# Bias of a fill as one wide matmul, fused VectorE operations, a late dense layer and a re-planned order in a four-layer graph kernel

## The reference, cut to what matters

```python
# layer 0: pairwise filters, then two dense layers
y = einsum('bjf,bijf->bif', rf, Wf * A)            # Wf: Gaussians of adj -> dense -> softplus -> dense
y = softplus(y @ Wd1 + bd1) - log 2
x = x + y @ Wd2.T + bd2
# layer 1: hyperbolic graph attention over all pairs i, j of a graph
h    = proj(mobius_add(mobius_matvec(W, h), bias))
xloc = logmap(h_i, h_j)                            # for each pair; needs artanh of a norm
att  = sigmoid(silu([logmap(h_i, h_i), xloc] @ w1.T + b1) @ w2.T)
s    = silu([.., sum_j att * xloc * adj] @ mlp_w1.T + b) @ mlp_w2.T + mlp_b2
x    = x + proj(expmap0(silu(logmap0(proj(expmap(s, h))))))
# layer 2: normalised adjacency times x, dense;  layer 3: message passing, dense
```

## Time and profile before

| | |
|---|---|
| runs | 2771.51, 2779.19, 2786.45 us, median 2779.19 |
| profiled execution | 2783.16 us, of which the span is 2781.3 |
| busy share of the span | PE 89%, DVE 80%, ACT 74%, POOL 64%, PEld 44% |
| mean granted clock of TensorE | 0.935 of full speed |

### The profile page before, as it was taken

One profiled execution on the slowest core, in us unless ns is written; L12 is line 12 of the kernel. 1 busy time (PEld: TensorE's weight loads), 2 busy tenths in 40 slices (PEclk: granted clock), 3 DMA queues, 4 the chain that ended last, 5 costly groups with the idle time before them and its releaser, 6 DMA issues. The chain is left out here.

```text
span 2781.3 us, 63446 instructions
## 1 busy us (share of the span) xinstructions
PE 2473.5 (89%) x25488; PEld 1229.5 (44%) x25488; DVE 2236.3 (80%) x3819; ACT 2066.1 (74%) x1938; POOL 1768.6 (64%) x1149
## 2 busy tenths in 40 slices
PE   4899999999999999999985588899898989898973
PEld 2333333333333333333334355455555555555543
DVE  6699898989989899898986756788888787874546
ACT  5888888888888888888853476767667777776641
POOL 0798898889989898898871344454545453555321
PEclk9999999999999999999995699999999999999976
DMA  8799898998989899999921466565555555576520
GB/s 232 172 200 202 194 198 195 201 201 192 203 194 201 193 202 199 196 197 197 199 68 56 86 122 126 100 125 101 126 101 117 106 108 112 104 115 110 75 53 19
DMA packets 312068, 410.29 MB, mean 148 GB/s; under 512 B 91488, under 2 KB 284640, under 8 KB 286688
## 3 DMA queue, kind: packets, MB, share of 16 engines
q1 hardware_dynamic: 311776, 406.23, 69.8%
HBM read 368.38 MB, written 35.65 MB: 145 GB/s over the span
## 5 line engine op out<-in xcount | busy, mean ns | idle before, releaser
L684 POOL TENSOR_TENSOR f_gate<-rfT,f_sq 128x1024 f32<-128x1024 f32 x512 | 1217.7, 2378 | 227.3 <-DVE f_prod L699 153.1
L617 PE MATMUL PS<-f_h,w_W2T 64*64 64x512 f32 x8192 | 998.9, 591 | 10.0 <-PE PS L617 1.9
L699 DVE SCALAR_TENSOR_TENSOR f_prod<-PS,b2l,f_gate 128x1024 f32<-128x1024 f32 x512 | 657.4, 1284 | 146.7 <-PE PS L617 110.9
L1192 ACT ACTIVATE a_silu<-PS,c_att_b 128x1024 f32<-128x1024 f32 x512 | 544.4, 1110 | 218.0 <-PE PS L1022 215.9
L579 ACT ACTIVATE f_h<-PS,c_b 128x1024 f32<-128x1024 f32 x512 | 556.3, 1113 | 167.3 <-PE PS L599 166.5
L691 DVE TENSOR_REDUCE yT<-f_prod 128x16 f32<-128x1024 f32 x512 | 618.8, 1209 | 0.0
L1334 POOL TENSOR_TENSOR a_outer<-a_by_i,a_by_j 128x256 f32<-128x256 f32 x512 | 355.3, 719 | 413.1 <-PE PS L1022 399.8
L617 PEld LDWEIGHTS PS<-f_h,w_W2T 64*64 64x64 f32 x8192 | 341.1, 133 | 561.4 <-issue 437.7
L599 PE MATMUL PS<-f_gauss,W1two 64*64 64x512 f32 x4096 | 546.1, 595 | 7.1 <-ACT f_gauss L566 4.8
L1022 PE MATMUL PS<-a_outer,a_rows 32*128 32x128 f32 x8192 | 395.0, 299 | 121.1 <-ACT a_silu L1192 82.6
L1022 PEld LDWEIGHTS PS<-a_outer,a_rows 32*128 32x128 f32 x8192 | 319.4, 197 | 339.5 <-issue 147.4
(11 more groups left out here) (244 smaller groups left out, 2288.5 us busy)
## 6 DMA issues: line engine op xcount, KB each, us to landing
f_gauss<-in_adj SPq DMA_DIRECT2D x128, 1024.0 KB, 11.6
f_sq<-adj_sq SPq DMA_DIRECT2D x256, 512.0 KB, 8.6
a_rows<-hw_d SPq DMA_DIRECT2D x1024, 64.0 KB
hw_d<-b_xc SPq DMA_DIRECT2D x16, 512.0 KB, 4.3
hw_d<-b_sq SPq DMA_DIRECT2D x16, 512.0 KB, 6.4
b_x<-in_x SPq DMA_DIRECT2D x8, 512.0 KB, 4.0
x_d<-b_x SPq DMA_DIRECT2D x8, 512.0 KB, 7.3
h_d<-b_h SPq DMA_DIRECT2D x8, 512.0 KB, 6.6
```

The source lines that it names most:

```text
L617: PE.matmul(post("message", c)[rows[b], n, :], W2T[rows[k], rows[fh]], hidden(c, n)[rows[k], b, :], start=not second, stop=bool(second)).t ...
L684: GP.tensor_tensor(by_pair(GATE[c % GATE_BUFS][:]), rf, by_pair(squares), ALU.mult).then_inc(s_gate, 1)
L699: V.scalar_tensor_tensor(PR[c % PR_BUFS][:], post("message", c).rearrange("p b n -> p (b n)"), b2l[:, c % 2:c % 2 + 1], GATE[c % GATE_BUFS ...
L1192: A.activation(SI[p % SI_BUFS][:], PS[:, first:first + 2, :].rearrange("p b n -> p (b n)"), ACT.Silu, bias=cols["att_b1"][:]).then_inc(s_s ...
```

## The change

- The filter stage no longer does the last group's dense layer. `flow_stage` does it: 16 matmuls on PE behind the y fills of lead(1) and two softplus activations on ACT behind the square of lead(1); `Wd1two` stays in memory for it.
- In `per_tile_and_bias` one matmul of 512 columns writes the bias of all 4 tiles, and the 4 tiles' matmuls accumulate on it. Its stationary operand is the first column of the identity, broadcast, so it is 128 partitions deep. `ones` shrinks to one column, broadcast where it is used (L1109).
- `series` loses its last addition of 1, which is folded into the operation that follows; `blend` has three operations and no mask buffer, where it had four; the pair chain loses its addition of 1.
- All ticks are new, and `SHIFT` moves single chains of the first and last groups.

```diff
-    posts.append(("layer", GROUPS - 1))
...
-        layer(GROUPS - 1)
...
 FILLS = {
-    "lead": (("y0", 18.875), ("y1", 21.5625), ("t0", 25.8125), ("t1", 25.8125), ("m0", 34.4375),
-             ("m1", 47.875), ("d", 47.875)),
-    "pair": (("h0", 3.1875), ("h1", 3.1875), ("g", 5.5), ("y", 5.5), ("r0", 8.4375), ("r1", 8.4375),
-             ("r2", 8.4375), ("r3", 12.125)),
+    "lead": (("y0", 19.75), ("y1", 19.75), ("t0", 23.4375), ("t1", 23.4375), ("m0", 33.1875),
+             ("m1", 44.4375), ("d", 44.4375)),
+    "pair": (("h0", 5.25), ("h1", 5.25), ("g", 5.25), ("y", 5.25), ("r0", 9.5), ("r1", 9.5), ("r2", 9.5),
+             ("r3", 11.6875)),
...
+SHIFT = {("lead", 0): -4.25, ("lead", 1): 8.875, ("lead", 2): 4.5, ("pair", 0): -3.1875, ("pair", 1): 4.125, ("mix", 6): -0.0625, ("mix", 7): 1.3125, ("last", 5): -0.1875, ("last", 6): -0.75, ("last", 7): 9.5}
...
         def per_tile_and_bias(n, lhs, rhs, bias, h):
             free(n)
+            PE.matmul(bank(n), ident[:, 0:1].broadcast_to([P, P]), bias[:].unsqueeze(1).broadcast_to([P, HALF_GT, P]),
+                      start=True, stop=True)
             for k in range(HALF_GT):
-                PE.matmul(bank(n)[:, k, :], ones[0:1, :], bias[0:1, :], start=True, stop=False)
-                last = PE.matmul(bank(n)[:, k, :], lhs(h * HALF_GT + k), rhs, start=False, stop=True)
+                last = PE.matmul(bank(n)[:, k, :], lhs(h * HALF_GT + k), rhs, start=False, stop=True,
+                                 skip_group_check=True)
...
+        def late_layer():
+            for fh in range(2):
+                for n in range(2):
+                    first = LATE_GROUP * BANK + n * BANK // 2
+                    for graph in range(2):
+                        for m in range(2):
+                            k_rows, m_rows = slice(graph * NODES, (graph + 1) * NODES), slice(m * NODES, (m + 1) * NODES)
+                            last = PE.matmul(PS[m_rows, 2 * graph + n, 0:BANK // 2], Wd1two[k_rows, fh, m_rows],
+                                             yT[k_rows, fh, first:first + BANK // 2], start=fh == 0, stop=fh == 1,
+                                             skip_group_check=True)
+                            if fh:
+                                last.then_inc(s_hb, 1)
...
+            if g == LATE_GROUP:
+                PE.wait_ge(s_hb, 3 + LAYER_PARTS + 2)
...
+            if g == 1:
+                late_layer()
...
+        def late_layer():
+            A.wait_ge(s_hb, 3 + LAYER_PARTS)
+            for graph in range(2):
+                A.activation(yT[:, :, LATE_GROUP * BANK:(LATE_GROUP + 1) * BANK]
+                             .rearrange("p n (t b i) -> p n t b i", b=2, i=NODES)[:, :, :, graph, :],
+                             PS[:, 2 * graph:2 * graph + 2, 0:BANK // 2].rearrange("p n (t i) -> p n t i", i=NODES),
+                             ACT.Softplus, bias=bd1[:]).then_inc(s_hb, 1)
...
-                ts(o, o, 1.0, ALU.add)
...
-            def blend(o, w, q, msk):
-                tt(w, w, o, ALU.subtract)
-                ts(msk, q, SMALL_SQ, ALU.is_ge)
-                tt(w, w, msk, ALU.mult)
-                tt(o, o, w, ALU.add)
+            def blend(o, w, q):
+                stt(w, w, 1.0, o, ALU.subtract, ALU.subtract)
+                stt(w, q, SMALL_SQ, w, ALU.is_ge, ALU.mult)
+                stt(o, o, 1.0, w, ALU.add, ALU.add)
...
-            tt(e1, e1, e2, MU)
+            stt(e1, e1, 1.0, e2, AD, MU)
...
-            yield 24.5
-            ts(bT[:], bT[:], 1.0, AD)
...
-            yield 33.375
+            yield -112.75
             tt(sF("sn3"), sF("n3"), sF("in3"), MU, gives=(f["clamp"], g))
-            yield 59.5625
+            yield -172.9375
             V.wait_ge(f["tanh3"], g + 1)
```

More of the change, by code:

```diff
@@ L662, in pe_program @@
                     ended += 1
-                    if posts[ended][0] == "layer":
+                    if ended < len(posts) and posts[ended][0] == "layer":
                         first_half(begun)
@@ L761, in run @@
     for slot in range(FIRST_SLOT, GROUPS + 3):
-        live += [Paced(chains[c](slot + ahead), slot * TICKS) for c, ahead in AHEAD.items() if 0 <= slot + ahead < GROUPS]
+        live += [Paced(chains[c](slot + ahead), slot * TICKS + SHIFT.get((c, slot + ahead), 0)) for c, ahead in AHEAD.items() if 0 <= slot + ahead < GROUPS]
         for tick in range(TICKS):
@@ L782, in fill_numbers, with flow_stage @@
     return numbers
-def flow_stage(nc, own, PS, d, W, WrlT, W3, rows, cols, ident, ones, same, by_a, by_m, w2sel, yT, norm, bX, d_x):
+def flow_stage(nc, own, PS, d, W, WrlT, W3, rows, cols, ident, ones, same, by_a, by_m, w2sel, yT, norm, bX, d_x, Wd1two,
+               bd1):
     V, A, PE, GP, SP = nc.vector, nc.scalar, nc.tensor, nc.gpsimd, nc.sync
@@ L1108, in pair @@
                 for r in (slice(0, NODES), slice(NODES, P)):
-                    last = PE.matmul(line(num["y"])[r, k * NODES:(k + 1) * NODES], ones[:, 0:NODES], bMX[:, k, r],
+                    last = PE.matmul(line(num["y"])[r, k * NODES:(k + 1) * NODES], ones[:].broadcast_to([P, NODES]), bMX[:, k, r],
                                      start=True, stop=True)
@@ L1517, in lead @@
             tt(sB("d4"), sB("d4"), sB("rstd"), MU)
-            yield -3.0625
+            yield 13.75
             V.wait_ge(b["ln"], g + 1)
             stt(sB("w"), sB("w"), 0.5, sB("zr"), MU, MU)
-            yield -163.3125
-            blend(sB("o"), sB("w"), sB("q"), sB("msk"))
-            yield -176.1875
+            yield -70.75
+            blend(sB("o"), sB("w"), sB("q"))
+            yield 24.875
             tt(sB("o"), sB("o"), sB("z"), MU)
@@ L1611, in pair @@
             ts(bden[:], bden[:], MIN_NORM, MA)
[L1612 removed]
+            yield 5.875
             recip(bden[:], bden[:], gives=(b["den"], g))
[L1614 removed]
+            yield -25.75
             stt(bq[:], bq[:], 0.0, bden[:], MA, MU, gives=(b["q"], g))
[L1616 removed]
+            yield -62.0625
             ts(bT[:], bq[:], 1.0 / 11, MU)
[L1618 removed]
+            for k, at in ((9, -223), (7, -88.5), (5, -265.875), (3, -77.75)):
                 yield at
                 stt(bT[:], bT[:], 1.0 / k, bq[:], AD, MU)
[L1621 to L1623 removed]
+            yield 21.9375
             V.wait_ge(b["z"], g + 1)
@@ L1631, in pair @@
             tt(by[:], by[:], bz[:], MU)
-            yield -36.4375
-            blend(bT[:], by[:], bq[:], bm[:])
-            yield -214.1875
+            yield -42.8125
+            blend(bT[:], by[:], bq[:])
+            yield -188.25
             tt(bT[:], bT[:], bden[:], MU, gives=(b["T"], g))
             tt(bm[:], bT[:], of_pairs(x2_1), MU, gives=(b["m"], g))
-            yield 26.1875
+            yield 31.3125
             stt(U[g % 3][:], bm[:], -1.0, bn[:], MU, MU, gives=(b["U"], g))
@@ L1735, in mix @@
             recip(sF("zi"), sF("zi"))
-            yield -128.125
+            yield -131.375
             series(sF("o"), sF("q"))
-            yield -6.25
+            yield -152.125
             V.wait_ge(f["ln"], g + 1)
             stt(sF("w"), sF("w"), 0.5, sF("zr"), MU, MU)
-            yield -188.375
-            blend(sF("o"), sF("w"), sF("q"), sF("msk"))
-            yield -250.5
+            yield -429.0625
+            blend(sF("o"), sF("w"), sF("q"))
+            yield -338.875
             tt(sF("o"), sF("o"), sF("z"), MU)
@@ L1816, in last @@
                 for h in range(2):
-                    yield {36: (-13.5625, -46.1875), 39: (-67.3125, 55.5)}[first][h]
+                    yield {36: (43.0625, 47.125), 39: (-85.0625, 52.8125)}[first][h]
                     n = num[f"{name}{h}"]
```

263 lines of the change are left out of this document (131 added, 132 removed), and 10 rows, old and new, of the table FILLS.

## The result

The changed kernel takes 2765.97 us (median of 10 runs, 2761.5 to 2781.5) against 2777.92 before (10 runs). The ratio is 0.9961, with an interval of 0.9942 to 0.9979: faster by 0.4%, or 12 us, where 75 were forecast and a range of 2665 to 2748 was given. The profiled execution took 2761.50 us, the shortest of its runs, with a span of 2759.6; so its profile stands 21.7 us under that of before, where the medians stand 12 apart.

The account below looks back on a forecast made before the run. Start and tail were taken as bound by chains, the attention middle by PE (88% busy). Start 16.3, bias 31, clock 17, b_h 7 and tail 4 sum to 75 us, giving 2704 us; range 2665 to 2748.

Parts of the forecast that it names:

- All other ticks: 0: Whole kernel: new ticks not covered by another term were put at 0 us gained or lost.
- rival A: Only start and tail gain; the bias matmul pays nothing or ACT takes the middle over: 2759 us, chance 0.13.
- Border and first y, 5.5 + 3.8: Start: moving the dense layer off the filter stage's end gains 5.5 us; shorter first y fills gain 3.8.
- First chain, 8.0 less 1.0: Start: first pair chain 8.0 us shorter, with lead(1) behind it; 1 us lost to the dense layer's work in lead(1).
- Bias in attention, 31 of 35: Attention: 26 halves of y and z fills get shorter on PE, 31 us gained, bounds 0 and 35.
- Clock, 17 of 35: Middle: TensorE's low-clock stretches at y and z fills given back by the new form, 17 us, bounds 0 and 35.
- Waits for b_h, 7 of 14.8: Attention: PE's waits before the turns of b_h shrink as h0's tick moves later, 7 us, between 0 and 14.8.
- Tail, 4: Tail: last group's z fills gain 5.0 us, less about 1 for fills k let in ahead: 4 us.
- Rival D: Slower: DVE waits for mix's third tanh, delaying the next b_h and PE's turns: 2800 us, chance 0.06.

Follow-up runs that it names:

- the aligned kernel: The changed kernel with its ones kept as a fifth column of norm, 32 bytes fewer, buffers back at the old remainder modulo 512: 2714.0 us, ratio 0.9756.
- a depth of one: The kernel before with only the bias edit, its 512-column bias matmul one partition deep in place of 128: 2717.5 us, ratio 0.9779.

## Why the prediction was wrong

The step that failed is the end of the sum for the middle. It closes with "All other ticks: 0" and has no term at all for memory: the change shrinks `ones` to one column and keeps `Wd1two`, and the prediction did not look at addresses. The wait for the loads of a_rows, which it took at its old 3.6 us, became 61.6, and the shift of the buffers by 32 bytes cost 52 us of time. The loads of a_rows stood in none of the rivals; rival A names the right place (the middle gives nothing, start and tail do) and nearly the right time, 2759, by a mechanism that wasn't there.

With the address put right and all else as changed the kernel takes 2714, inside the range and 10 from the forecast of 2704. That it comes so near is partly luck. The sum had 57 us for what the bias edit gives and 18 for all the rest; measured are 64 for the bias edit alone and 1 for the rest on top of it (2714.0 for 2715.1). By point, with the sizes from the profiles of the changed and of the aligned kernel:

- *Border and first y, 5.5 + 3.8.* Right and a little small: the first matmul came at 1455.11 (6.0 earlier), and the two halves took 6.1 us, not 7.8 (5.5 gained). The sum doubled the warm length for the lower clock, but the second half already ran partly at the full one. (The "16 pairs" of the prediction are 8 pairs of 16 matmuls; nothing in the sum hangs on it.)
- *First chain, 8.0 less 1.0.* The first set began 17.7 us earlier (1543.71 for 1561.44), as said. What failed is what follows from it. On ACT's timeline of the changed kernel:

```profile
1549.09 0.21 ACT L1256 ACTIVATE b_small<-b_small 128x8 f32<-128x8 f32 x1 [7.80 <-DVE b_small L1456]
1549.32 1.28 ACT L1259 ACT_TABLE_LOAD   x1
1552.97 0.21 ACT L1259 ACTIVATE b_small<-b_small 128x8 f32<-128x8 f32 x1 [2.37 <-DVE b_small L1452]
1553.20 1.28 ACT L1214 ACT_TABLE_LOAD   x1
1554.50 2.12 ACT L1214 ACTIVATE a_silu<-PS,c_att_b 128x1024 f32<-128x1024 f32 x2
```

The logarithm and the tanh of lead(1), which was moved behind the pair chain, stand on ACT ahead of the first silu. It comes at 1554.50; before, it came at 1563.55. Of 17.7 us, 9 were left at the first silu, and 11 at the first silu of the second group (1677.6 for 1688.9). With the old ticks, aligned, attention starts 4 us later (1547.90), and its first silu comes 4.5 us earlier (1550.01).

- *Bias in attention, 31 of 35.* Right: a half took 3.2 us and now takes 1.85 or, alone and before `dots`, 1.95, so 26 halves save 33 to 36 us of PE. With the clock's part the edit alone gains 64 us, of which the sum had 3.8 + 31 + 17 + 5 = 57.
- *Clock, 17 of 35.* Taken at half, and it was nearly whole: 32 us came back with the bias edit alone, and 24 at a depth of one. That the alternation of the two shapes is what lets the clock fall fits the fills shown above; depth by itself has at most the difference. In the changed kernel nearly nothing came back (78 us for 80), since PE often goes on at the lower clock behind a wait for rows; aligned, it is 54.
- *Waits for b_h, 7 of 14.8.* All 14.8 went, but through the new ticks, which on balance gained nothing: against the old ones they lose 6 us with the new bias matmuls, where the intervals overlap, and 24 with the old. So this term and "other ticks 0" should have been about -6 together in this kernel.
- *Tail, 4.* 6.2 in the changed kernel and 5.5 aligned; right.
- *Rival D.* Between 1600 and 2600 us DVE waits 6.8 us in all for the third tanh, six times, once 4.6; no wait of PE for b_h came of it, as put.

The same 32 bytes cost 14 us in the kernel before, 31 with the bias edit, 37 with all edits at the old ticks, 52 in the changed kernel and 54 in it with the old bias matmuls. One picture fits: the loads have some slack, a slower load uses it up, and a faster PE, or a plan that issues the loads later, leaves less of it. The last of the five is the slowest kernel of all, so the plan counts in it and not the pace. The sizes were measured; the picture is argued and was not tested, say by a third buffer for the loads.

The fastest kernel found is the one with all edited operations, the old ticks and the aligned buffers: 2708.4 us, 2.6% faster than before.

## What to carry to other kernels

A constant made smaller moves every buffer allocated behind it; before costing such a change at nothing, write down the start addresses of the buffers that the steady transfers fill, and compare their remainders, here modulo 512 (a multiple of 64 was not enough). The sign in the profile is a DMA share that rises at the same bytes, whatever the order of the transfers; here it was 0.67 for 0.58 at 108 GB/s. And the time of a first event on one engine is a gain only if the next engine isn't held in order by something else: follow the moved chain through each queue that it passes.

## What the runs showed of the hardware

- With the loads of a_rows going to a buffer that begins 32 bytes past a multiple of 512 (in one kernel 64), the queue's packet time per MB was 0.58 to 0.62% of a 1000 us window, in eight kernels; in the eight kernels without the offset it was 0.53 to 0.55%. The kernel's time followed, by 14 to 54 us. The longer time sits in the pieces of 1024 bytes, 117 to 129 ns for 99 to 105. The two kernels that tell most have the pad ahead of a_rows and behind it:

```profile
q1 hardware_dynamic: 229136, 110.22, 64.3%
```

```profile
q1 hardware_dynamic: 235410, 113.12, 60.6%
```

- Eight matmuls of 128 columns, alternately 1 and 128 partitions deep, took 3.2 us at full clock; one of 512 columns and four of 128 took 1.85 to 1.95, for the same number of columns. With the 512-column one a single partition deep it was 2.05, the tile matmuls of z have a mean of 315 ns where the full depth has 275, and the kernel's time is the same within its interval.
- Sixteen such alternating matmuls on end went with a granted clock below 1 in all 20 places of attention (seven before, 13 in all but the bias edit, aligned), with PE busy throughout; two fills of the wide form on end in none of 20 (seven and 13).
